# A GNN block: second convolution split by even and odd taps twice instead of once, groups of graphs in pairs, loops unrolled

## What is computed

```python
h = jnp.maximum(_layernorm(x, axis=-1), 0.0)
# block, x below is h:
h1 = relu(bn1(conv1d(xc, conv1_w, 0)))            # 1 tap, 128 x 128; xc is x with channels first
x_conv = relu(bn2(conv1d(h1, conv2_w, 8)) + xc)   # 17 taps, each a 128 x 128 matrix
s = x @ w_se.T + b_se                             # 3 columns
A = exp(-squared_distances(s)) * mask             # 128 x 128 for each graph
x_nmp = A @ relu(x @ w_msg.T + b_msg)
gi = concat(x_conv, x_nmp) @ w_ih.T + b_ih        # GRU gates r, z, n
gh = x @ w_hh.T + b_hh
r, z = sigmoid(gi_r + gh_r), sigmoid(gi_z + gh_z)
out = (1 - z) * tanh(gi_n + r * gh_n) + z * x
```

## Time and profile before

| what | us |
|---|---|
| median of 3 runs (lowest, highest) | 342.02 (340.93, 342.55) |
| profiled execution, span | 341.0 |
| TensorE busy | 327.4 |
| VectorE busy | 259.7 |
| ScalarE busy | 167.4 |
| GpSimd busy | 61.0 |

### The profile page before, as it was taken

The page is one execution under the profiler, slowest core; times in us unless marked ns, Lnnn a source line. Parts: engine busy times, 40 slices in busy tenths (PEclk is TensorE's granted clock), DMA queues, the critical chain, the costliest instruction groups (busy, mean ns, idle before and its releaser), DMA issues.

```text
span 341.0 us, 7050 instructions
## 1 busy us (share of the span) xinstructions
PE 327.4 (96%) x2293; PEld 301.9 (89%) x2293; DVE 259.7 (76%) x832; ACT 167.4 (49%) x302; POOL 61.0 (18%) x81
## 2 busy tenths in 40 slices
PE   3889999999999999999999999999999999999994
PEld 3779799898989989898999989898998989899993
DVE  4788988787887878787887878788787878787335
ACT  1256555454546536454544555354653645464413
POOL 5403103012030302103030301203030210302010
PEclk9979999999999999999999999999999999999997
...
DMA packets 52130, 14.66 MB, mean 43 GB/s; under 512 B 34549, under 2 KB 51973, under 8 KB 51989
## 3 DMA queue, kind: packets, MB, share of 16 engines
...
...
## 4 chain that ended last, share of the span: by engine, by line
PE 92%; DVE 3%; DMA 2%; ACT 1%; issue 1%; SPq 0%; DVEq 0%
PE bank L880 26%; PE bank L882 25%; PE bank L881 25%; PE bank L968 4%; PE bank L939 4%; PE bank L923 2%; PE bank L1012 2%; DMA c_nat<-in_L_gnn_conv_w 2%; PE bank L958 1%; PE bank L1038 1%; PE bank L1026 0%; PE bank L947 0%; ACT h_hi L395 0%; DVE bn_ms L790 0%; DVE bn_scale L788 0%
## 5 line engine op out<-in xcount | busy, mean ns | idle before, releaser
L880 PE MATMUL bank<-a_hi,w_hi 128*128 128x248 f32 (+3 forms) x416 | 125.2, 301 | 0.2 <-DVE a_lo L620 0.2
L881 PE MATMUL bank<-a_lo,w_hi 128*128 128x248 f32 (+3 forms) x416 | 118.5, 285 | 0.0
L882 PE MATMUL bank<-a_hi,w_lo 128*128 128x248 f32 (+3 forms) x416 | 118.5, 285 | 0.0
L880 PEld LDWEIGHTS bank<-a_hi,w_hi 128*128 128x128 f32 x416 | 79.5, 191 | 1.1 <-ACT w_hi L385 0.5
L881 PEld LDWEIGHTS bank<-a_lo,w_hi 128*128 128x128 f32 x416 | 79.7, 192 | 0.7
L882 PEld LDWEIGHTS bank<-a_hi,w_lo 128*128 128x128 f32 x416 | 79.4, 191 | 0.0
L339 POOL TENSOR_TENSOR h_q<-h_s,q 128x256 f32<-128x256 f32 x16 | 11.9, 743 | 233.7 <-ACT h_s L440 233.7
L722 DVE SCALAR_TENSOR_TENSOR hn<-t_r,hh_n 128x512 f32<-128x512 f32 (+1 forms) x17 | 11.2, 660 | 30.5 <-ACT t_r L472 30.5
L472 ACT ACTIVATE t_r<-bank,gru_b 128x512 f32<-128x512 f32 (+1 forms) x17 | 11.3, 663 | 45.5 <-PE bank L882 45.5
L402 ACT ACTIVATE a_f<-bank,bn_shift,bn_scale 128x512 f32<-128x512 f32 x16 | 12.5, 778 | 27.9 <-PE bank L882 27.9
L880 PE MATMUL bank<-h_hi,w_hi 128*128 128x512 f32 (+1 forms) x66 | 25.8, 391 | 0.0
...
## 6 DMA issues: line engine op xcount, KB each, us to landing
...
```

The lines of the kernel that those rows point to most:

```text
L880: pe.matmul(out, w_hi[:, mat, :], hi, start=start, stop=False)
L881: pe.matmul(out, w_hi[:, mat, :], lo, start=False, stop=False)
L882: last = pe.matmul(out, w_lo[:, mat, :], hi, start=False, stop=stop)
```

## The change

Groups are taken in pairs: 8 pairs of 8 graphs (PB = 8, NP = 8), and all loops are written out in Python, with no hardware loop. Element work that is 512 columns wide is done once for each half k of a pair; small work (dist_sides, moments, rstd) once for the pair with twice the elements.

The second convolution is split twice. The output of conv1 is kept in four phases (node modulo 4) and five sums of them (C0, C1, S0, S1, CS), made by VectorE in `phase_sums`. Nine products with 41 matrices, each on a quarter of the columns (8 graphs by 30 or 32), take the place of three with 26: "g", "g0", "g1" common to both output parities, "a", "a0", "a1" for even and "b", "b0", "b1" for odd nodes. One-letter products go to half of bank B_CA, the others to the halves of B_CB. The combination is on ScalarE (`g_scaled`) and VectorE (`common_part`, `residual`, `parity_part`, `conv_out`), in place of GpSimd's `conv_parts` and VectorE's `conv_even` and `conv_odd`. `h_shifted` is gone: z_times_h reads h_f, and the factor 0.5 moves to `result`, which now adds into the tile of x in place.

There are 51 weight matrices instead of 35, in 14 chunks instead of 10. GpSimd and VectorE form differences of taps (g_d, f_nat, f_d) out of the taps as loaded. The left side of the distances is placed by four ScalarE copies (`dist_sides_out`) instead of VectorE's `dist_left`. x tiles lie in four slots of a pair each, two of them in the place of the raw weights, and are loaded once these are no longer needed. conv1_w is loaded first on ScalarE's queue.

The diff, cut to its core (lines with a sign are added; what they replace is in the functions printed above):

```diff
+        PHASE, C0, C1, S0, S1, CS = 0, 4, 5, 6, 7, 8
+        SHIFTS4, SHIFTS5 = (-2, -1, 0, 1), (-2, -1, 0, 1, 2)
+        PRODUCTS = {"g": (CS, -1, SHIFTS4, 0), "g0": (S1, -1, SHIFTS4, 0), "g1": (S0, 0, SHIFTS5, 1),
+                    "a": (C0, -1, SHIFTS4, 0), "a0": (PHASE + 0, 0, SHIFTS5, 0), "a1": (PHASE + 2, 0, SHIFTS5, 1),
+                    "b": (C1, -1, SHIFTS4, 0), "b0": (PHASE + 1, 0, SHIFTS5, 0), "b1": (PHASE + 3, 0, SHIFTS5, 1)}
+        FIRST_MAT, CONV1, count = {}, 0, 1
+        for name, (_, _, shifts, _) in PRODUCTS.items():
+            FIRST_MAT[name] = count
+            count += len(shifts)
...
+            pool.tensor_tensor(g_d[:, 0:4, :], taps_nat[:, 3:16:4, :], taps_nat[:, 1:14:4, :], ALU.subtract
+                               ).then_inc(comb_g, 1)
...
+            pool.tensor_tensor(g_d[:, 5:8, :], taps_nat[:, 3:12:4, :], taps_nat[:, 5:14:4, :], ALU.subtract
+                               ).then_inc(comb_g, 1)
+            pool.tensor_scalar(g_d[:, 4, :], taps_nat[:, 1, :], -1.0, None, ALU.mult).then_inc(comb_neg, 1)
+            pool.tensor_copy(f_nat[:, 0, 0, :], taps_nat[:, 0, :]).then_inc(comb_copy, 1)
+            pool.tensor_copy(f_nat[:, 1, 8, :], taps_nat[:, 16, :]).then_inc(comb_copy, 1)
+            for f in range(2):
+                pool.wait_ge(comb_f, f + 1)
+                pool.wait_ge(comb_copy, 2 + f)
+                pool.tensor_tensor(f_d[:, f, 0:4, :], f_nat[:, f, 0:8:2, :], f_nat[:, f, 1:8:2, :], ALU.subtract
+                                   ).then_inc(comb_d, 1)
+                pool.tensor_copy(f_d[:, f, 4, :], f_nat[:, f, 8, :]).then_inc(comb_copy, 1)
+                pool.wait_ge(comb_d, 2 * f + 1)
+                pool.wait_ge(comb_copy, 3 + f)
+                pool.tensor_tensor(f_nat[:, f, 2:9:2, :], f_nat[:, f, 2:9:2, :], f_nat[:, f, 1:8:2, :], ALU.subtract
+                                   ).then_inc(comb_d, 1)
+            for t in range(1, NP):
+                norm_rstd(t + 1, slice(0, PB))
...
+            def phase_sums(t):
+                dve.wait_ge(a1f_ready, 2 * t + 2)
+                wait(dve, a1hi_ready, 2 * t)
+                wait(dve, a1lo_ready, 2 * t)
+                v0, v1 = VOFF, VOFF + VN
+                dve.tensor_tensor(a1_f[:, S0, :, v0:v1], a1_f[:, 1, :, v0:v1], a1_f[:, 2, :, v0:v1], ALU.add
+                                  ).then_inc(sums_ready, 1)
+                dve.tensor_tensor(a1_f[:, S1, :, v0 - 1:v1], a1_f[:, 3, :, v0 - 1:v1], a1_f[:, 0, :, v0:v1 + 1],
+                                  ALU.add).then_inc(sums_ready, 1)
+                dve.tensor_tensor(a1_f[:, C0:C1 + 1, :, v0 - 1:v1], a1_f[:, 2:4, :, v0 - 1:v1],
+                                  a1_f[:, 0:2, :, v0:v1 + 1], ALU.add).then_inc(sums_ready, 1)
+                dve.wait_ge(sums_ready, 4 * t + 2)
+                dve.tensor_tensor(a1_f[:, CS, :, v0 - 1:v1], a1_f[:, S0, :, v0 - 1:v1], a1_f[:, S1, :, v0 - 1:v1],
+                                  ALU.add).then_inc(sums_ready, 1)
...
+            def common_part(s):
+                dve.wait_ge(product_done["g1"], s + 1)
+                dve.wait_ge(gs_ready, s + 1)
+                wait(dve, h_added, 2 * s)
+                if s == 0:
+                    dve.wait_ge(wT_done, CHUNKS_G1)
+                dve.scalar_tensor_tensor(both(t_sum), both(bank[B_CB][:, :]), bn_scale[:, 1:2], twice(g_s), ALU.mult,
+                                         ALU.add).then_inc(t_ready, 1)
+            def residual(s, e):
+                dve.wait_ge(t_ready, s + 1)
+                wait(dve, convf_ready, 2 * (s - 1) + e + 1)
+                dve.tensor_tensor(both(pre[e]), both(t_sum), by_pair(h_f[s % 2][:, :])[:, e], ALU.add
+                                  ).then_inc(h_added, 1)
+            def parity_part(s, e):
+                dve.wait_ge(product_done["ab"[e]], s + 1)
+                dve.wait_ge(h_added, 2 * s + e + 1)
+                dve.scalar_tensor_tensor(both(pre[e]), twice(bank[B_CA][:, 0:VC]), bn_scale[:, 1:2], both(pre[e]),
+                                         ALU.mult, ALU.add).then_inc((a_added, b_added)[e], 1)
+            def conv_out(s, e):
+                dve.wait_ge(product_done[("a1", "b1")[e]], s + 1)
+                dve.wait_ge((a_added, b_added)[e], s + 1)
+                wait(dve, convlo_ready, 2 * s)
+                wait(dve, convhi_ready, 2 * s)
+                if s == 0:
+                    dve.wait_ge(wT_done, chunks_for("a0"))
+                    dve.wait_ge(comb_f, 2)
+                dve.scalar_tensor_tensor(by_pair(conv_f)[:, e], both(bank[B_CB][:, :]), bn_scale[:, 1:2],
+                                         both(pre[e]), ALU.mult, ALU.add).then_inc(convf_ready, 1)
...
+            dve.tensor_tensor(f_nat[:, 0, 1:9, :], taps_nat[:, 2:17:2, :], taps_nat[:, 1:16:2, :], ALU.subtract
+                              ).then_inc(comb_f, 1)
+            phase_sums(0)
             weights_low(2)
             dist_sides(0)
+            a1_low(0)
             weights_low(3)
+            dve.tensor_tensor(f_nat[:, 1, 0:8, :], taps_nat[:, 0:15:2, :], taps_nat[:, 1:16:2, :], ALU.subtract
+                              ).then_inc(comb_f, 1)
+            adj_transposed(0, 0)
+            adj_transposed(0, 1)
...
+            def iteration(s):
+                t = s + 1
+                ahead = t < NP
+                if s > 0:
+                    n_hidden(s - 1, 1)
+                    n_argument(s - 1, 1)
+                    z_times_h(s - 1, 1)
+                if ahead:
+                    h_low(t, 0)
+                    h_low(t, 1)
+                if s > 0:
+                    z_times_n(s - 1, 1)
+                    gates_out(s - 1, 1)
+                else:
+                    common_part(0)
+                    residual(0, 0)
+                    residual(0, 1)
+                    weights_low(8)
+                    weights_low(9)
+                if ahead:
+                    messages(t)
+                if s == 0:
+                    weights_low(10)
+                    weights_low(11)
+                if ahead:
+                    dist_sides(t)
+                if s > 0:
+                    common_part(s)
+                    residual(s, 0)
+                    residual(s, 1)
+                if ahead:
+                    phase_sums(t)
+                parity_part(s, 0)
+                if ahead:
+                    adj_transposed(t, 0)
+                    adj_transposed(t, 1)
+                if s > 0:
+                    result(s - 1, 0, OUT_BANKS[0])
+                    result(s - 1, 1, OUT_BANKS[1])
+                conv_out(s, 0)
+                if s == 0:
+                    weights_low(12)
+                    weights_low(13)
+                if ahead:
+                    masked_edges(t, 0)
+                    masked_edges(t, 1)
+                parity_part(s, 1)
+                if s + 2 < NP:
+                    x_stats(s + 2, 0)
+                    x_stats(s + 2, 1)
+                    x_moments(s + 3, PB * (s + 3), slice(0, PB))
+                conv_out(s, 1)
+                if ahead:
+                    nmp_low(t, 0)
+                conv_low(s, 0)
+                conv_low(s, 1)
+                if ahead:
+                    a1_low(t)
+                    nmp_low(t, 1)
+                n_hidden(s, 0)
+                n_argument(s, 0)
+                z_times_h(s, 0)
+                if s + 2 < NP:
+                    x_normed(s + 2, 0)
+                z_times_n(s, 0)
+                gates_out(s, 0)
+                if s + 2 < NP:
+                    x_normed(s + 2, 1)
+            for s in range(NP):
+                iteration(s)
+            first, second = column_parts(True)
+            end = (NP - 1, 1)
+            result(NP - 1, 0, END_OUT_BANKS[0])
+            n_hidden(*end, *first)
...
+            def conv2_product(s, name, first=0, stop=5):
+                kind, begin, shifts, side = PRODUCTS[name]
+                order = sorted(shifts, key=abs)
+                dst = bank[B_CA if len(name) == 1 else B_CB][:, side * VC:(side + 1) * VC]
+                dst = dst.rearrange("p (b v) -> p b v", b=PB)
                 if first == 0:
+                    if s == 0:
+                        split_done(chunks_for(name))
+                    if name == "g":
+                        pe.wait_ge(a1lo_ready, 2 * s + 1)
+                        pe.wait_ge(a1hi_ready, 2 * s + 1)
+                        if s == 0:
+                            pe.wait_ge(msb_ready, 1)
+                        wait(pe, b_added, s)
+                    elif name == "g0":
+                        wait(pe, convf_ready, 2 * s)
+                    elif name == "a":
+                        pe.wait_ge(gs_ready, s + 1)
+                    elif name == "a0":
+                        pe.wait_ge(a1lo_ready, 2 * s + 2)
+                        pe.wait_ge(a1hi_ready, 2 * s + 2)
+                        pe.wait_ge(t_ready, s + 1)
```

(64 more changed lines are left out.)

1301 lines of the change are left out of this document (605 added, 696 removed).

## The result

The changed kernel takes 337.86 us (median of 13 runs, 336.38 to 340.64) against 341.74 for the kernel before on the same chip: a ratio of 0.9907, 95% interval 0.9881 to 0.9932. Beside the experiments further down it was timed once more: 338.36, ratio 0.9881 (0.9846 to 0.9916). So it is about 1% faster. The forecast was 328.3, 4% faster: the sign and the range (319 to 340) hold, the size is 9.6 us off. The profiled execution has a span of 336.1.

A forecast was written before the change was run, and what follows sets the result against it. TensorE, busy 96% of the span, was taken as the bound. First pair ending at 79.5, six pairs 210.6, last pair 28.6 and end 8.6 sum to 327.3; plus 1.0, 328.3 us. Own range 323 to 334, full range 319 to 340.

The forecast's parts named there:

- The bound: Steady pair: TensorE's queue sets it, at 35.1 us where two groups took 39.06.
- eight may cost 0.126 ... I take 0.124: conv2 on TensorE: 0.124 us per 256-column matmul in eight blocks of 32, 15.0 us a pair, 3.7 less.
- The upper bound, 0.127: conv2 on TensorE: highest price allowed for a 256-column matmul, in us; the lower bound was 0.118.
- VectorE's walk: Steady pair: VectorE's queue against TensorE's, 31.1 us of work, no TensorE wait, closest hand-over conv_out(0) to b0 with 0.9.
- rival 2: VectorE's late steps: blocks of 32 or four-element steps cost 1.5 times, pair about 39.5, time 355, slower; chance 0.10.
- VectorE idles only some 3 us: Steady pair: idle time left to VectorE in 35.1 us, with TensorE never waiting.
- Rival 1: VectorE becomes the bound, still faster: pair 36.7 (34.2 work, 2.5 waits), time 338; chance 0.22.
- Rivals 3 and 4: Start and pair 0 cost 8 us less, 320, chance 0.11; TensorE's products 0.136 us each whatever their columns, 342, chance 0.05.
- The start: Before the first "g" product: it starts at 28.9 us, 3.1 of it VectorE's loss to GpSimd's operations.
- Pair 0: First pair: 38.9 us of TensorE work, 3.0 for the low clock, 8.7 of waits, ending at 79.5.
- another 2.7: First pair: us of TensorE waits for x_normed(1), masked_edges, conv_low, late hh_n and gate_r, besides b's 6.0.
- The end: Behind TensorE's last product: n_hidden at +1.2 because result(7,0) stands ahead of it, 8.6 us instead of 6.3.

The follow-up runs named there:

- e14_light: Changed kernel with VectorE's two transposes of adj cut from 512 to 32 columns in all pairs but the first; 339.42 us (single run).
- e6_dup: Changed kernel with each residual step of VectorE done twice; 352.28 us, ratio 1.0322 to the kernel before.
- e7_nopool: Changed kernel with GpSimd's second-level tap differences (f_d and those within f_nat) cut to 2 columns; 337.77 us (single run).
- after_again: The changed kernel with nothing altered, timed once more beside the experiments as their baseline; 338.36 us, ratio 0.9881 to the kernel before.

## Why the prediction was right or wrong

The forecast of 13.7 us less became 3.9. The sum missed in the steady pair (3.5 us in six, 3 of them the price of a matmul), in the waits and the work of pair 0 (3.9), in the last pair (0.5), and by 1.9 behind TensorE's last product and outside the span, which say little of the kernel. What TensorE does and who waits for whom in the steady pair came as forecast; the sizes did not.

- **The bound, right.** TensorE sets the steady pair, as e14_light shows: the pair keeps its 35.65 us with less work on VectorE.
- **The matmul's price, wrong by 0.5 us a pair (3 of the 9.6 us).** The step "eight may cost 0.126 ... I take 0.124" took the average of 93 matmuls from the number of blocks. It goes by where the blocks start: 81 at 0.130 and 12 at 0.120, and 240 columns at 0.118 instead of 0.114, 15.5 us for 15.0. The upper bound, 0.127, was too low: the four blocks of 64 in the earlier trace rows hid most of the cost, at most one part in 17 where it is now one in nine. The rule of 2.5 ns per matmul in the Trainium skill ("TensorE: Matmul & The Clock Gate", Back-to-back issue gap) gives 109 ns for 256 columns and knows only their number; with contiguous operands the trace comes nearest, 118.
- **VectorE's walk, right in the outcome, wrong in the sizes.** It has no late hand-over, as forecast, but b0's reserve is 0.2 instead of 0.9 us, and its work is 32.0 instead of 31.1. What the charge left out is the stride of four elements: residual takes 1.02 to the next step (two in 199.67 to 201.71) and conv_out 0.98, where 0.61 was charged to each, 1.6 us over four steps. No run takes the stride away by itself; other steps of 512 elements in the same pair take 0.60 to 0.66.

```profile
206.58 1.14 DVE L687 SCALAR_TENSOR_TENSOR place<-bank,bn_scale,place 128x512 f32<-128x512 f32 x1
207.56 0.67 DVE L647 TENSOR_TENSOR edge_m<-adj_T,edge 128x512 f32<-128x512 f32 x1
```

That is the mechanism of rival 2, at 1.6 to 1.7 times the price, but for four steps and not for the 9 us of them that the rival counted (phase_sums, a1_low and parity_part have their usual prices). "VectorE idles only some 3 us" was measured (3.6); that these idle microseconds aren't slack was missed. At 2.1 us more, e6_dup, the slower side was real.
- **Rival 1, wrong, and its number luck.** Its 338 is what came out, but it has VectorE as the bound and the pair at 36.7, with 34.2 of work and 2.5 of waits. VectorE's own limit is below 35.65, near 34.7, and 6 of the 9.6 us that make its number lie outside the steady pairs.
- **Rivals 3 and 4, wrong.** The start and pair 0 were not cheaper, and TensorE's price per product fell with the columns.
- **The start, right.** 28.75 for 28.9, with the holding by GpSimd (L577, L582) seen; other profiles have up to 29.97. e7_nopool shows 2.2 of the 3.1 us charged for it as the cost of these operations; the rest of the term was right by chance or is spread over others.
- **Pair 0, 3.9 too cheap.** b's wait came as worked out (5.66 in the list, 5.9 between starts, for 6.0). The step "another 2.7" for the other waits failed: they are 4.9, counted from start to start with the usual distance taken off (3.6 of it is in the list). 1.8 of it is for x_norm, 1.5 one that no step had named, conv1(1, 1) for the messages' addition (L599), 1.1 for conv_low and 0.5 in two gaps of the GRU products; masked_edges, which the step names, cost none. The low clock cost 1.4 and 1.9 instead of 1.5 and 1.5, against the same products in a steady pair. What is left is work, some 40.5 for 38.9: 0.5 is the matmul's price, 0.6 are first matmuls behind other work, of which pair 0 has 14 and a steady pair seven, each some 0.08 us dearer, and 0.2 is that out_transposes, which pair 0 lacks, take 0.8 and not 1.0; some 0.3 is not resolved.
- **The end, right, though the profile has 1.1 more.** n_hidden at +1.25 came as forecast (+1.2), and from it to the last `result` it takes 4.6 us as in the earlier trace rows. TensorE, idle for 3.7 us, does the last transposes at half clock (1.46 us for four), but that doesn't lengthen these 4.6. The 1.1 lie behind the last `result`, 3.8 us to the span's end where the kernel before has 2.7 (338.27 in the earlier trace rows to 341.0). Profiles of other edits, all with this same last store, have 2.6 to 5.0, and after_again, the unchanged kernel, has 2.7, its end 8.6.
- **Outside the span**, 1.8 us instead of 1.0, 0.8 of the miss. The forecast took the 1.0 from a median and one span; in the runs beside the experiments it is 2.0 to 2.2 for the kernel before.

What stays open: why blocks 40 elements apart cost 2% more than blocks 36 apart, some 0.3 us of pair 0, and what makes the last store and the first loads scatter by one or two microseconds.
